# Dissolving a layer norm and routing stage into its neighbours, in a kernel of two attention and expert layers

## The chip, the cores and the metric

The kernel runs on one core of a Trainium2 chip. The metric is the device time of one execution in microseconds (us), the median of several runs. The core has five engines that run side by side, each from an instruction queue of its own and tied to the others by semaphores: TensorE (PE in the profile), VectorE (DVE), ScalarE (ACT), GpSimd (POOL) and SyncE (SP), which here only issues DMAs.

## What is computed

Two layers on `x` (8 x 256 rows of 256) with a context of the same shape; float32 throughout.

```python
x = x + _L0_xattn_ref(ctx_1024, _layernorm(x, axis=-1), ...)   # 16 heads of 64, 512 keys
x = x + _L0_ffn_ref(_layernorm(x, axis=-1), ...)               # the part around the change
x = x + _L1_xattn_ref(_layernorm(x, axis=-1), ctx_1024, ctx_1024, ...)
x = x + _L1_ffn_ref(_layernorm(x, axis=-1), ...)

def _L0_ffn_ref(...):                # x: 2048 rows of 256, 16 experts, F = 512
    logits = x @ w_router.T
    _, top_idx = jax.lax.top_k(logits, 1)
    mask = jax.nn.one_hot(top_idx, E).sum(axis=1)
    scores = jax.nn.sigmoid(logits) * mask
    masked_inputs = scores.T[:, :, None] * x[None, :, :]
    gate_up = jnp.einsum('eth,ehf->etf', masked_inputs, gate_up_proj)
    gate, up = jnp.split(gate_up, 2, axis=-1)
    expert_out = jnp.einsum('etf,efh->eth', up * silu(gate), down_proj)
    shared = silu(x @ w_gate.T) * (x @ w_up.T) @ w_down.T
    return shared + expert_out.sum(axis=0)
```

## The kernel before

`program` (L2116) runs stages one after the other, each a block of its own, with the semaphores cleared in between: `attend_latents`, `norm_and_route`, `run_mixture`, `attend_context`, `norm_and_gate`, `choose_and_run`. `x` lives in SBUF as 16 tiles of 128 rows; a batch is two tiles.

Products that need near float32 precision are made "threefold": each operand is split into a high part in fp32r (a copy by ACT) and a low part (the rest, by a subtraction on DVE or POOL), and three products are summed: high by high, high by low, low by high.

**`attend_latents`** (L67) goes through 8 batches of 8 steps, a step for each pair of heads; `batches` (L764) unrolls batches 0, 1, 6 and 7 and loops over 2 to 5. The order of work of each engine is written out by hand in its `step`. On PE a step makes the scores of four tiles (L297, L298), turns the exponentials (L307), projects k, q and v of what comes next (L255), and attends for the pair before (L321, L325). On DVE it takes four negative maxima (`maximum`, L603), the low part of k (L597) and of q (L590), copies of turned tiles (`set_odd`, L618), and the output of a pair (`set_out`, L625, L627). After each of the four maxima there is a slot, `between(r, j)`, for one of the 19 parts of `prepare`, which normalises the next batch: statistics, then an inverse root by Newton steps on small tiles, every instruction chained to the one before by a semaphore (`link`). The 19 parts fill the slots of steps 0 to 3 and three of step 4; the rest of step 4 and steps 5 to 7 are empty. In steps 4 and 5 `fill` (L582) follows slot 4 (PE turns the inputs for it, L333). At the end of step 2 `project_out` and `add` (L632) add the batch before to `x`; PE waits for `added` ahead of the q projection in step 3.

**`norm_and_route`** (L774) takes statistics of all 16 tiles, the root on ACT, and then per batch: normalise (DVE L729), turn (PE L741), copy (DVE L748), router logits in float32 (PE L836), a copy of the normalised rows (ACT L807), and the high and low parts `xT_h` (ACT L753) and `xT_l` (POOL L760). At its start it loads the weights of the shared expert and splits them (ACT L822, POOL L799).

**`run_mixture`** (L871) begins with three of the four groups (512 rows each) of the shared expert (EARLY = 3), in 12 steps `shared(n)`: products for gate and up of 6 matmuls each (L1028), silu on ACT, `hidden` on DVE (L1265), its high part on ACT (L1133) and low part on DVE (L1267); after each four steps comes `down` (48 matmuls, L1040; it starts in the step after), then `add`. Meanwhile DVE works out the routing in five parts, `route(0)` ahead of step 0 and `route(1)` to `route(4)` behind steps 0 to 3: part 0 finds the chosen expert (`hot_set`), PE counts (`count`, after step 0), part 3 gives each row its place (`row_set`), part 4 the expert of each block (`blocks_set`). ACT weighs the rows with their score, four tiles behind each of steps 0 to 3. POOL then scatters the rows of each tile to DRAM (L999), and SP loads weights for block 0 at `blocks_set`, for block 1 when `hidden_set` is 8, rows of three blocks when all is scattered, weights of block 2 when `hidden_set` is 12. Then 31 blocks of experts follow: turn rows (L1062), `expand` (L1069), `contract` (L1079).

## Time and profile before

| | us |
|---|---|
| median of 3 runs | 1676.8 |
| lowest and highest | 1675.89, 1679.48 |
| the profiled execution | 1679.78 |
| its span, first to last instruction | 1678.1 |
| TensorE busy | 1479.7 (88% of the span) |
| VectorE busy | 1017.5 (61%) |
| ScalarE busy | 879.1 (52%) |
| GpSimd busy | 458.8 (27%) |

The span is shorter than the execution by what lies around the program. Busy times of PE are modelled from pipelined matmuls, so a busy PE isn't one at its peak. The page has a line with the TensorE clock that the throttle granted, in 40 slices of the span; it is at full speed except around four stretches, one of them at 729 to 770 us. A row of the timeline reads: start, length, engine, line, operation, output <- inputs, form, number of instructions merged, and in brackets the idle time before it and what ended it.

### The profile page before, as it was taken

The page shows a single profiled execution, that of the slowest core. Times are in us where ns is not written, and L with a number is a line of the kernel's source. Part 1 is how long each engine was busy: PE and PEld are TensorE (multiplying, and loading weights), DVE is VectorE, ACT ScalarE, POOL GpSimd, SP SyncE. Part 2 cuts the span into 40 slices and gives each one's busy share as a digit, 9 for nine tenths or more (in the row PEclk, how much of TensorE's full clock was granted, in tenths as well). Part 3 has the DMA queues.
Part 4 walks back from the last instruction along what each step waited for, and adds up shares of the span by engine and source line. Part 5 has one row for each costly group of instructions (what it writes and reads, how often), then busy time and mean ns, then how long its engine had stood idle before and what let it go on. Part 6 is the DMA issues. An engine that isn't in the chain of part 4 may idle for free. (4 is left out here: it accounts for less than half of the span.)

```text
span 1678.1 us, 28402 instructions
## 1 busy us (share of the span) xinstructions
PE 1479.7 (88%) x9884; PEld 1201.2 (72%) x9884; DVE 1017.5 (61%) x2142; ACT 879.1 (52%) x2200; POOL 458.8 (27%) x395
## 2 busy tenths in 40 slices
PE   4899999999999999958999996699999629999996
PEld 3678777777777778747888885365655518888885
DVE  5877777777777876755311115377777654444452
ACT  2676767676767777835211113366666214445442
POOL 6110101010101010033200006222322015777874
PEclk9999999999999999977999998599999659999998
DMA  3300000000000000012489883000000223445442
GB/s 115 108 14 1 14 1 14 2 14 2 14 2 14 1 1 1 1 38 98 135 296 318 300 287 60 19 14 7 12 3 2 88 81 101 119 121 126 122 116 33
DMA packets 72255, 118.17 MB, mean 70 GB/s; under 512 B 6864, under 2 KB 52944, under 8 KB 72112
## 3 DMA queue, kind: packets, MB, share of 16 engines
q1 hardware_dynamic: 61408, 99.66, 18.4%
q0 software_dynamic: 10704, 16.65, 4.9%
q8 instruction: 83, 1.36, 0.3%
q14 instruction: 60, 0.49, 0.1%
HBM read 97.68 MB, written 18.61 MB: 69 GB/s over the span
## 5 line engine op out<-in xcount | busy, mean ns | idle before, releaser
L435 ACT ACTIVATE a_p<-a_s,a_negmax 128x512 f32<-128x512 f32 x256 | 176.0, 688 | 157.6 <-DVE a_negmax L603 115.9
L603 DVE TENSOR_REDUCE a_negmax<-a_s 128x1 f32<-128x512 f32 x256 | 176.1, 688 | 47.0 <-PE a_s L298 36.8
L207 POOL TENSOR_TENSOR a_o_l<-a_o,a_o_h 128x256 fp32r<-128x256 f32 x64 | 47.0, 735 | 559.8 <-ACT a_o_h L460 559.8
L1495 ACT ACTIVATE h_probs<-h_scores,h_negmax 128x256 f32<-128x256 f32 x256 | 117.8, 473 | 88.6 <-DVE h_negmax L1662 88.6
L307 PEld LDWEIGHTS a_t<-ident,a_p 128*128 128x128 f32 x1024 | 121.1, 140 | 52.9 <-issue 17.9
L307 PE MATMUL a_t<-ident,a_p 128*128 128x128 f32 x1024 | 157.5, 277 | 0.7 <-DVE a_pT L618 0.7
L1907 POOL TENSOR_TENSOR n_w_l<-n_raw,n_w_h 128x768 fp32r<-128x768 f32 x64 | 118.3, 1849 | 74.7 <-ACT n_w_h L1950 74.7
L597 DVE TENSOR_TENSOR a_k_hl<-a_k_p,a_k_hl 64x512 fp32r<-64x512 f32 x128 | 88.1, 688 | 71.6 <-ACT a_k_hl L418 70.5
L325 PE MATMUL a_out_p<-a_pT,a_v 128*64 128x256 f32 x1024 | 124.7, 386 | 0.0
L297 PE MATMUL a_s<-a_k_hl,a_q_hh 128*128 128x512 f32 x256 | 108.5, 424 | 8.9 <-ACT a_p L435 7.2
L1662 DVE TENSOR_REDUCE h_negmax<-h_scores 128x4 f32<-128x1024 f32 x64 | 78.1, 1221 | 55.3 <-PE h_scores L1589 55.3
L2088 DVE TENSOR_TENSOR n_hidden<-n_up,n_silu 128x512 f32<-128x512 f32 x64 | 44.3, 692 | 97.9 <-PE n_up L1992 93.6
L1600 PEld LDWEIGHTS h_turned<-ident,h_probs 128*128 128x128 f32 x512 | 55.8, 143 | 66.1 <-issue 48.0
L298 PE MATMUL a_s<-a_k_hl,a_q_l 128*128 128x512 f32 x256 | 101.3, 396 | 0.0
L412 ACT ACTIVATE a_q_hh<-a_q_p 64x256 fp32r<-64x256 f32 x256 | 95.9, 375 | 2.3
L325 PEld LDWEIGHTS a_out_p<-a_pT,a_v 128*64 128x64 f32 x1024 | 67.8, 136 | 38.4 <-issue 10.7
L2091 DVE TENSOR_TENSOR n_hid_l<-n_hidden,n_hid_h 128x512 fp32r<-128x512 f32 x64 | 63.3, 989 | 44.7 <-ACT n_hid_h L1971 44.7
L618 DVE COPY a_pT<-a_t 128x512 f32<-128x512 f32 x128 | 87.8, 686 | 2.6 <-PE a_t L307 0.7
L1600 PE MATMUL h_turned<-ident,h_probs 128*128 128x128 f32 x512 | 73.6, 286 | 13.5 <-DVE h_probsT L1672 13.4
L1966 ACT ACTIVATE n_silu<-n_gate 128x512 f32<-128x512 f32 x64 | 38.3, 598 | 84.2 <-PE n_gate L1992 84.2
L1334 DVE TENSOR_TENSOR e_hidden<-m_up,e_silu 128x512 f32<-128x512 f32 x31 | 21.4, 692 | 100.3 <-PE m_up L1069 100.3
L255 PE MATMUL a_v_p<-a_w_h,a_kvT_h 128*128 128x256 f32 x256 | 77.8, 304 | 4.8 <-POOL a_kvT_l L202 3.7
(325 smaller groups left out, 4294.3 us busy)
## 6 DMA issues: line engine op xcount, KB each, us to landing
e_w_in<-in_L_ffn_gate_up_proj SPq DMA_DIRECT2D x31, 1024.0 KB, 7.1
n_raw<-in_L_ffn_w SPq DMA_DIRECT2D x64, 384.0 KB, 3.0
e_w_out<-in_L_ffn_down_proj SPq DMA_DIRECT2D x31, 512.0 KB, 5.2
rows_in<-a_zeros SPq DMA_DIRECT2D x1, 3968.0 KB, 14.6
e_rows<-rows_in SPq DMA_DIRECT2D x31, 128.0 KB, 5.0
rows_out<-e_result POOLq DMA_DIRECT2D x31, 128.0 KB, 4.8
x<-in_x SPq DMA_DIRECT2D x8, 256.0 KB, 2.8
a_ctx_in<-in_ctx SPq DMA_DIRECT2D x8, 256.0 KB, 3.1
```

Of the source, the lines that this page charges most:

```text
L297: pe.matmul(scores[j % 2][:, :], q_hh[r % 2][:, h, rows], k_hl[r % 2][h][:, :], start=True, stop=False)
L298: pe.matmul(scores[j % 2][:, :], q_l[r % 2][:, h, rows], k_hl[r % 2][h][:, :], start=False, stop=True).then_inc(s_done, 1)
L307: ins = pe.transpose(turned_p[j % 2][:, c, :], probs[j][:, c * P:(c + 1) * P], g.ident[:, :])
L325: ins = pe.matmul(out_p[h * DH:(h + 1) * DH, 0, :], v[r // 2 % 2][:, c, at:at + DH], probsT[r % 2][h][:, c, :], start=(c == 0), stop=(c == ...
L412: ins = act.activation(q_hh[r % 2][half, h, :], q_p[halves[h], 0:S], ACT.Copy, scale=QSCALE)
L435: act.activation(probs[j][:, :], scores[j % 2][:, :], ACT.Exp, bias=negmax[:, j:j + 1], accum_out=total[:, r % 2, j % 2, j // 2:j // 2 + 1 ...
L597: ins = dve.tensor_tensor(k_hl[r % 2][h][halves[1 - h], :], k_p[half, :], k_hl[r % 2][h][half, :], ALU.subtract)
L603: dve.tensor_reduce(negmax[:, j:j + 1], scores[j % 2][:, :], AX.X, ALU.max, negate=True).then_inc(max_set, 1)
L618: dve.tensor_copy(probsT[r % 2][j // 2][:, :, P:2 * P], turned_p[1][:, :, :]).then_inc(odd_set, 1)
L1495: ins = act.activation(probs[s % 4][:, j, :], scores[s % 2][:, j // 2, j % 2, :], ACT.Exp, bias=negmax[:, s % 4, j:j + 1], accum_out=total ...
L1600: ins = pe.transpose(turned_p[i][:, j, c, :], probs[s % 4][:, 2 * i + j, c * P:(c + 1) * P], g.ident[:, :])
L1907: pool.tensor_tensor(w_l[c % RAWS][:, :], raw[c % RAWS][:, :], w_h[c % RAWS][:, :], ALU.subtract).then_inc(wl_set, 1)
```

## The change

The stage `norm_and_route` is gone, and its work is spread. In `attend_latents` each batch's final rows are also written to a tile `done` (an addition more), and `measure`, in nine parts, takes mean and inverse root of them in the slots that `prepare` leaves: slot 4 of step 4 and the slots of steps 5 and 6 of the next batch; for the last batch at the end. SP loads the shared expert's weights into the spare tiles of the attention. In `run_mixture` ACT and POOL split the weights, DVE normalises (`apply`), PE turns (`turn_x`) and makes the logits, threefold in fp32r instead of float32 (`find_logits`, 6 matmuls for each tile), ACT and DVE take the high and low parts, all between the products of steps 0 to 3. The logits lie in the PSUM tile that `down` writes too. `route(0)` to `route(4)` move behind steps 3 to 7, `count` behind `down(0)` in step 4, the weighing of rows to steps 4 to 7 and the split of the next attention's weights to steps 8 to 11.

```diff
-raw = [sb(f"a_raw{i}", [P, 3 * KC * N // 2]) for i in range(2)]
+raw = g.spare
...
+done, next_stats, next_mv = sb("a_done", [P, 2, D]), sb("a_next_stats", [P, 2, 6]), sb("a_next_mv", [P, 2, 2])
+next_var, next_tmp, next_guess = sb("a_next_var", [P, 2]), sb("a_next_tmp", [P, 2]), sb("a_next_guess", [P, 2], I32)
...
+        sp.wait_ge(w_ready, PIECES + OUT_PIECES)
+        for i, (w, name) in enumerate(zip(g.shared_raw, ("gate", "up"))):
+            sp.dma_start(w, io[f"L0_ffn_w_{name}_T"].rearrange("(c p) n -> p c n", p=P)).then_inc(stored, 16)
+        down_dram = io["L0_ffn_w_down_T"].rearrange("(i c p) n -> p i c n", i=2, p=P)
+        for i, w in enumerate(g.shared_raw[2:]):
+            sp.dma_start(w, down_dram[:, i]).then_inc(stored, 16)
-        sp.wait_ge(stored, 16)
+        sp.wait_ge(stored, 16 * 5)
     def _(pool):
...
     def _(dve):
-        PARTS = 19
+        PARTS, MEASURES = 19, 9
         def seed_root(n):
...
+        def measure(b, part):
+            at = bass.ds(2 * b, 2)
+            rstd_of = g.rstd[:, at]
+            if part == 0:
+                for t in range(2):
+                    ins = dve.bn_stats(next_stats[:, t, :], done[:, t, :])
+                link(ins)
+            elif part == 1:
+                for t in range(2):
+                    ins = dve.bn_aggr(next_mv[:, t, :], next_stats[:, t, :])
+                link(ins)
+                dve.tensor_copy(g.mean[:, at], next_mv[:, :, 0])
+                link(dve.tensor_scalar(next_var[:, :], next_mv[:, :, 1], EPS, None, ALU.add))
+            elif part == 2:
+                link(dve.tensor_scalar(next_guess[:, :], next_var[:, :].bitcast(I32), 1, None, ALU.logical_shift_right))
+                link(dve.tensor_scalar(next_guess[:, :], next_guess[:, :], -1, 0x5f3759df, ALU.mult, ALU.add))
+            else:
+                src = next_guess[:, :].bitcast(F32) if part < 5 else rstd_of
+                if part % 2:
+                    link(dve.tensor_tensor(next_tmp[:, :], src, src, ALU.mult))
+                    link(dve.tensor_tensor(next_tmp[:, :], next_tmp[:, :], next_var[:, :], ALU.mult))
+                else:
+                    link(dve.tensor_scalar(next_tmp[:, :], next_tmp[:, :], -0.5, 1.5, ALU.mult, ALU.add))
+                    link(dve.tensor_tensor(rstd_of, src, next_tmp[:, :], ALU.mult))
         def low_q(b, r):
...
         def add(b):
-            rows = g.x[:, bass.ds(2 * b, 2), :]
-            dve.tensor_tensor(rows, rows, q_p[:, :].rearrange("p (t d) -> p t d", t=2), ALU.add).then_inc(added, 1)
+            rows, sums = g.x[:, bass.ds(2 * b, 2), :], q_p[:, :].rearrange("p (t d) -> p t d", t=2)
+            link(dve.tensor_tensor(done[:, :, :], rows, sums, ALU.add))
+            dve.tensor_tensor(rows, rows, sums, ALU.add).then_inc(added, 1)
         def step(b, bp, first, last):
             def between(r, j):
-                if last < 2 and 4 * r + j < PARTS:
-                    prepare(b + 1, 4 * r + j)
+                if 4 * r + j < PARTS:
+                    if last < 2:
+                        prepare(b + 1, 4 * r + j)
+                elif not first and 4 * r + j < PARTS + MEASURES:
+                    measure(b - 1, 4 * r + j - PARTS)
             for r in range(PAIRS):
...
+        for part in range(MEASURES):
+            measure(NB - 1, part)
...
-def norm_and_route(nc, g, io):
...
 def run_mixture(nc, g, io):
...
-raw = [sb(f"g_raw{i}", [P, KC, D]) for i in range(4)]
+raw = [w[:, i * KC * D:(i + 1) * KC * D].rearrange("p (c n) -> p c n", c=KC) for w in g.spare for i in range(2)]
+router, router_h, router_l = (sb(f"r_router{i}", [P, KC, E], dt) for i, dt in enumerate((F32, F32R, F32R)))
+SPLITS = [(g.shared_h[i][:, :, :], g.shared_l[i][:, :, :], g.shared_raw[i]) for i in range(2)]
+SPLITS += [(g.shared_h[2][:, 2 * i:2 * i + 2, :], g.shared_l[2][:, 2 * i:2 * i + 2, :], g.shared_raw[2 + i]) for i in range(2)]
+logits = sum_ps[1][:, 0, :].rearrange("p (t e) -> p t e", e=E)
+r_in, sh_set, sl_set, rh_set, rl_set = sem("r_in"), sem("s_sh_set"), sem("s_sl_set"), sem("r_rh_set"), sem("r_rl_set")
+x_normed, x_turned, x_high, x_low, logits_done = sem("x_normed"), sem("x_turned"), sem("x_high"), sem("x_low"), sem("r_logits_done")
...
+        sp.dma_start(router[:, :, :], io["L0_ffn_w_router_T"].rearrange("(c p) e -> p c e", p=P)).then_inc(r_in, 16)
+        sp.wait_ge(sl_set, 4)
         for dst, name in zip(raw, ("Wq", "Wk", "Wv", "Wo")):
...
     def _(pool):
+        for i in range(len(SPLITS)):
+            high_w, low_w, raw_w = SPLITS[i]
+            pool.wait_ge(sh_set, i + 1)
+            pool.tensor_tensor(low_w, raw_w, high_w, ALU.subtract).then_inc(sl_set, 1)
+            if i == 1:
+                pool.wait_ge(rh_set, 1)
+                pool.tensor_tensor(router_l[:, :, :], router[:, :, :], router_h[:, :, :], ALU.subtract).then_inc(rl_set, 1)
...
+        def turn_x(b):
+            pe.wait_ge(x_normed, b + 1)
+            wait(pe, x_low, b - 1)
+            for kc in range(KC):
+                for t in range(2):
+                    ins = pe.transpose(small[b % 2][:, kc, t * P:(t + 1) * P],
+                                       g.xn[:, 2 * b + t, kc * P:(kc + 1) * P], g.ident[:, :])
+            ins.then_inc(x_turned, 1)
+        def find_logits(b):
+            pe.wait_ge(x_low, b + 1)
+            for t in range(2 * b, 2 * b + 2):
+                at = slice(t * P, (t + 1) * P)
+                passes = [(x, w, kc) for kc in range(KC)
+                          for x, w in ((g.xT_h, router_h), (g.xT_h, router_l), (g.xT_l, router_h))]
+                for k, (x, w, kc) in enumerate(passes):
+                    ins = pe.matmul(logits[:, t, :], x[:, kc, at], w[:, kc, :], start=(k == 0), stop=(k == len(passes) - 1))
+            if b == NB - 1:
+                ins.then_inc(logits_done, 1)
         def shared(n, first):
+            if n % FC == 0 and n // FC * 2 < NB:
+                pe.wait_ge(x_low, 2 * (n // FC) + 2)
+            if n == 0:
+                pe.wait_ge(sl_set, 1)
             product(gate_ps[n % 2], 0, n, gated)
+            if n < NB // 2:
+                if n == 0:
+                    pe.wait_ge(rl_set, 1)
+                find_logits(2 * n)
+                if 2 * n + 2 < NB:
+                    turn_x(2 * n + 2)
+            if n == 0:
+                pe.wait_ge(sl_set, 2)
             product(up_ps[n % 2], 1, n, upped)
+            if n < NB // 2:
+                find_logits(2 * n + 1)
+                if 2 * n + 3 < NB:
+                    turn_x(2 * n + 3)
             if n % FC == 0 and n > first:
+                if n == FC:
+                    pe.wait_ge(sl_set, 4)
+                    pe.wait_ge(hot_set, 1)
         def count():
...
+        turn_x(0)
+        turn_x(1)
         for n in range(FC * EARLY):
             shared(n, 0)
-            if n == 0:
+            if n == FC:
...
         for n in range(FC * EARLY, FC * GROUPS):
-        down(GROUPS - 1)
+        if EARLY < GROUPS:
+            down(GROUPS - 1)
         for b in range(NB):
...
+        def high_w(i):
+            act.activation(SPLITS[i][0], SPLITS[i][2], ACT.Copy).then_inc(sh_set, 1)
+        def take_high(b):
+            act.wait_ge(x_turned, b + 1)
+            act.activation(g.xT_h[:, :, b * S:(b + 1) * S], small[b % 2][:, :, :], ACT.Copy).then_inc(x_high, 1)
+        high_w(0)
+        act.wait_ge(r_in, 16)
+        act.activation(router_h[:, :, :], router[:, :, :], ACT.Copy).then_inc(rh_set, 1)
+        take_high(0)
+        high_w(1)
+        take_high(1)
+        high_w(2)
+        high_w(3)
         for n in range(FC * EARLY):
-            if n == 0:
+            if 2 * n + 2 < NB:
+                take_high(2 * n + 2)
+            if n == 4:
-            if n == 0:
+            if 2 * n + 3 < NB:
+                take_high(2 * n + 3)
+            if n == 4:
-            if n < 4:
-                weigh_rows(range(n * NT // 4, (n + 1) * NT // 4))
-            else:
-                if n == 4:
+            if n in range(4, 8):
+                weigh_rows(range((n - 4) * NT // 4, (n - 3) * NT // 4))
+            elif n >= 8:
+                if n == 8:
-                if n - 4 < len(splits):
-                    act.activation(splits[n - 4][0][:, :, :], raw[n - 4][:, :, :], ACT.Copy).then_inc(wh_set, 1)
+                if n - 8 < len(splits):
+                    act.activation(splits[n - 8][0][:, :, :], raw[n - 8], ACT.Copy).then_inc(wh_set, 1)
         for j in range(BLOCKS):
...
         def route(part):
             if part == 0:
-                dve.tensor_reduce(top[:, :], g.logits[:, :, :], AX.X, ALU.max).then_inc(top_set, 1)
+                dve.wait_ge(logits_done, 1)
+                dve.tensor_reduce(top[:, :], logits, AX.X, ALU.max).then_inc(top_set, 1)
-                link(dve.tensor_tensor(hot[:, :, :], g.logits[:, :, :], along(top[:, :], E), ALU.is_equal))
+                link(dve.tensor_tensor(hot[:, :, :], logits, along(top[:, :], E), ALU.is_equal))
...
         def scale_queries():
...
+        def apply(b):
+            for t in range(2 * b, 2 * b + 2):
+                ins = dve.tensor_scalar(g.xn[:, t, :], g.x[:, t, :], g.mean[:, t:t + 1], g.rstd[:, t:t + 1],
+                                        ALU.subtract, ALU.mult)
+            ins.then_inc(x_normed, 1)
+        def take_low(b):
+            dve.wait_ge(x_high, b + 1)
+            at = slice(b * S, (b + 1) * S)
+            dve.tensor_tensor(g.xT_l[:, :, at], small[b % 2][:, :, :], g.xT_h[:, :, at], ALU.subtract).then_inc(x_low, 1)
         def shared(n):
+            if 2 * n + 2 < NB:
+                take_low(2 * n + 2)
+                if 2 * n + 4 < NB:
+                    apply(2 * n + 4)
...
+            if 2 * n + 3 < NB:
+                take_low(2 * n + 3)
+                if 2 * n + 5 < NB:
+                    apply(2 * n + 5)
         def add(grp):
...
-        route(0)
+        for b in range(2):
+            apply(b)
+        for b in range(2):
+            take_low(b)
+        for b in range(2, 4):
+            apply(b)
         for n in range(FC * EARLY):
-            if n < 4:
-                route(n + 1)
-            elif n == 4:
+            if n in range(3, 8):
+                route(n - 3)
+            elif n == 8:
             if n % FC == 1 and n > FC:
...
-attend_latents(nc, g, io)
-clear_semaphores(nc)
-with ExitStack() as ctx:
+g.mean, g.rstd = keep(whole, "mean", [P, g.NT]), keep(whole, "rstd", [P, g.NT])
+ctx = ExitStack()
+with ctx:
+    g.spare = [keep(ctx, f"spare{i}", [P, 3 * g.KC * g.S]) for i in range(2)]
+    half = g.KC * g.F
+    g.shared_raw = [w[:, 0:half].rearrange("p (c n) -> p c n", c=g.KC) for w in g.spare]
+    g.shared_raw += [w[:, half:].rearrange("p (c n) -> p c n", c=2) for w in g.spare]
+    attend_latents(nc, g, io)
+    clear_semaphores(nc)
...
-        g.logits = keep(inner, "logits", [P, g.NT, g.E])
-        norm_and_route(nc, g, io)
-        clear_semaphores(nc)
```

## Rows read from the trace of the kernel before

**Rows 1.** Table of windows: stretch, us, busy time (instructions) per engine, clock, DMA share, GB/s
```profile
637.00:728.00 91.00, 85.94 (x617) 69.42 (x616) 57.43 (x108) 60.22 (x151) 8.03 (x11) 1.00 0.00 1
729.00:764.00 35.00, 20.19 (x96) 19.78 (x96) 23.91 (x62) 15.47 (x29) 17.21 (x11) 0.55 0.14 46
764.00:788.00 24.00, 19.39 (x74) 14.72 (x75) 16.71 (x50) 15.63 (x29) 4.14 (x7) 0.86 0.21 66
764.00:828.00 64.00, 57.16 (x291) 48.33 (x292) 30.01 (x71) 26.49 (x48) 22.38 (x24) 0.90 0.40 134
1070.00:1094.00 24.00, 22.15 (x79) 15.24 (x79) 8.23 (x10) 11.82 (x40) 9.78 (x10) 0.50 0.03 11
```

**Rows 2.** Timeline of DVE over the two changes of block
```profile
728.34 0.69 DVE L632 TENSOR_TENSOR x<-x,a_q_p 128x512 f32<-128x512 f32 x1 [7.30 <-PE a_q_p L255]
729.95 5.33 DVE L711 BATCH_NORM_STATS2 c_stats<-x 128x6 f32<-128x256 f32 x16 [0.92 <-PEq L2109]
735.31 1.17 DVE L714 BATCH_NORM_AGGREGATE c_mv<-c_stats 128x2 f32<-128x6 f32 x16
...
764.64 0.42 DVE L1218 TENSOR_REDUCE r_top<-logits 128x16 f32<-128x256 f32 x1 [3.69 <-PEq L2109]
```

**Rows 3.** Timeline of PE in the two stages after the attention
```profile
757.46 1.73 PE L836 MATMUL c_logit<-c_router,c_full 128*128 128x16 f32 x8
...
765.20 0.63 PE L1028 MATMUL m_gate<-xT_l,shared_h 128*128 128x512 f32 x1
765.63 0.63 PE L1028 MATMUL m_gate<-xT_h,shared_l 128*128 128x512 f32 x1
...
771.29 0.40 PE L1028 MATMUL m_gate<-xT_h,shared_l 128*128 128x512 f32 x1
...
786.00 0.39 PE L1040 MATMUL m_sum<-shared_h,s_hid_h 128*128 128x256 f32 x1 [1.80 <-DVE s_hid_l L1267]
...
827.91 0.39 PE L1062 MATMUL m_small<-ident,e_rows 128*128 128x128 f32 x2
```

**Rows 4.** Timeline of DVE: two chained small instructions of `prepare`
```profile
499.38 0.17 DVE L512 TENSOR_SCALAR a_var<-a_mv 128x2 f32<-128x2 f32 x1
499.58 0.17 DVE L513 TENSOR_SCALAR a_guess<-a_var 128x2 int32<-128x2 int32 x1
```

**Rows 5.** Timeline of PE: attends in steps 0, 1, 2, 5, 7 of batch 5, 0 of 6
```profile
471.85 0.38 PE L321 MATMUL a_out_p<-ident,a_inverses 128*128 128x128 f32 x2
...
482.97 0.41 PE L321 MATMUL a_out_p<-ident,a_inverses 128*128 128x128 f32 x2 [0.66 <-DVE a_pT L618]
...
493.29 0.41 PE L321 MATMUL a_out_p<-ident,a_inverses 128*128 128x128 f32 x2 [0.65 <-DVE a_pT L618]
...
529.38 0.41 PE L321 MATMUL a_out_p<-ident,a_inverses 128*128 128x128 f32 x2 [0.66 <-DVE a_pT L618]
...
549.52 0.38 PE L321 MATMUL a_out_p<-ident,a_inverses 128*128 128x128 f32 x2
...
558.90 0.38 PE L321 MATMUL a_out_p<-ident,a_inverses 128*128 128x128 f32 x2
```

**Rows 6.** Timeline of DVE ahead of `set_out`: step 5 of batch 5, and a clean step
```profile
530.23 0.86 DVE L590 SCALAR_TENSOR_TENSOR a_q_l<-a_q_p,a_q_hh 64x256 fp32r<-64x256 f32 x2 [0.35 <-ACT a_q_hh L412]
...
531.72 0.42 DVE L625 COPY a_inverse_T<-a_out_p 128x256 f32<-128x256 f32 x1
...
655.58 0.42 DVE L625 COPY a_inverse_T<-a_out_p 128x256 f32<-128x256 f32 x1 [0.57 <-PE a_out_p L325]
```

**Rows 7.** Timeline of POOL (split of weights, scatter), and a wait of SP's queue
```profile
734.64 6.95 POOL L799 TENSOR_TENSOR shared_l<-c_raw,shared_h 128x1024 fp32r<-128x1024 f32 x3 [12.34 <-ACT shared_h L822]
...
784.23 1.18 POOL L999 DMA_INDIRECT rows_in<-xn,row_of  x1 [18.56 <-DVE row_of L1248]
...
804.21 0.97 POOL L999 DMA_INDIRECT rows_in<-xn,row_of  x1 [0.30 <-issue]
...
SPq L964 <- DMA rows_in<-xn,row_of: 6.0, 1, 6.0
```

83 lines of the change are left out of this document (4 added, 79 removed).

## The prediction

> **What bounds the kernel now.** I read four views: the page for the stages, the table of windows for clock and busy shares, the timeline of each engine from 464 to 560 us and 640 to 830 us, and the waits of the stage from 764 us. The first attention is bound by TensorE: in its last 91 us PE is busy 86 at full clock [rows 1]. The stage the change removes is not: between 729 and 764 us PE is busy 20 of 35 us, at a mean clock of 0.55, only turning tiles and making logits [rows 1]. It starts 0.9 us after the last addition of the attention ends and hands over at 764.6 [rows 2]. The early groups of the shared expert run from there to 827.9, where the first rows of the experts are turned [rows 3]; PE is busy 57 of 64 us there [rows 1]. The gain can only come from 729.0 to 827.9; the bill is sent partly to the attention.
>
> **Removed.** From 729.03 (728.34 + 0.69) to 764.6 is 35.6 us: a block change of 0.92, then 34.6 us of stage [rows 2]. The block change stays, so the removal is worth 34.6.
>
> **Added at the end of the attention.** The last batch has nothing to hide under. First a second addition of 128x512 (into `done`), chained: 0.7, as the row of the existing one [rows 2]. Then nine parts: two statistics (16 took 5.33, so 0.7 for two [rows 2]), the aggregation with copy and the variance (0.6), two seed instructions and twelve Newton instructions, all chained, 0.20 apart [rows 4]: 2.8. Sum 4.9 us on the path.
>
> **Added inside the attention.** DVE's chain there is: attend (L321/L325) on PE, then `set_out`, `set_odd`, `maximum` of the next head pair, exp and two copies on ACT, `low_k`, `set_odd`, and the next attend. In a step with nothing extra attends are 9.38 apart (549.52 to 558.90), and this is also PE's own work [rows 5]. What happens when DVE gets small chained parts in all four slots is in the trace, since `prepare` does this: 471.85 to 482.97 is 11.12 and 482.97 to 493.29 is 10.32, so 1.74 and 0.94 are lost; four Newton parts take 4 x 0.42 = 1.7 us of DVE, and the step loses over half of it [rows 5]. The first slot lies in a wait of DVE and is free; slots 2 and 3 share 0.57 us of idle time ahead of `set_out` (655.58), slot 4 has no cover [rows 6]. Check: 0.84 - 0.57 + 0.42 = 0.69 against 0.94.
> The new parts go to slot 4 of step 4, and all slots of steps 5 and 6. Those steps are already late: 529.38 to 549.52 is 20.14 for two, 1.4 over, with `fill` in slot 4 and the turning of inputs on PE [rows 5]. Per batch in the loop: slot 4 of step 4, two statistics, 0.8, in full. Step 5: first slot free (a wait for ACT); slots 2 and 3, 0.84, less the 0.35 that DVE waits before `low_q` at 530.23 (ahead of 531.72 there is no idle left) [rows 6], so 0.5; slot 4, 0.45: 0.95. Step 6 by the measured 0.94, less some slack of the clean step 7: 0.8. The chained extra addition in step 2 delays the next `maximum` by 0.75; the chain of step 3 has about 0.25 to spare: 0.5. That is 3.05 for each of the four looped batches. The unrolled ones carry no address arithmetic; batches 1 and 6 I take at 2.4, batch 7, which has no `prepare` and starts from clean steps, at 1.9. Sum 12.2 + 4.8 + 1.9 = **19 us**. Bounds: if only the statistics show, 0.5 x 7, some 4 us; if every chained pair costs its time, 7 x 3.7, 26. I stay near the upper middle since rows 5 measure just such parts. The four weight DMAs on SP stand before the load of batch 2 and wait for a split long done by then; nothing is queued behind them that is due soon: 0.
>
> **The new front of the expert stage**, t from its start. Before, gate product 0 starts at 0.1. Now it waits for `x_low` 2. ACT: weight copy, router (landing some 2.3, bounded by the 2 of a small load and 6), copy of batch 0 (to 3.3), weight copy 1 (to 4.4), copy of batch 1 (5.0); DVE takes the low part to 5.8. POOL's low parts (6.95 for three, 2.3 each [rows 7]) end at 3.4 and 6.7 and are behind that for `gate` and just in time for `up`. So gate 0 starts at **5.9**.
> Steps 0 to 3 each have 12 matmuls of 512 columns: 0.43 apart at the low clock [rows 3], about half that at the full (0.23 with the gap), 5.1 or 2.8 in all, plus 24 logit matmuls of 16 columns, and 8 transposes in the first three (0.9 to 1.9 us). The logit matmuls in fp32r aren't in the trace; fp32 ones are 1.73 for 8 at the low clock, 0.22 each, 0.11 at the full [rows 3]; no less than 0.05, a quarter of the former, since these pass fp32 once instead of four times (an estimate). I take 0.075, 1.8 a step at the full clock. DVE gets per step, beside the pair of 0.69 us, two low parts (0.69 each) and two normalisations (0.7 each), 4.9 us, so PE, at 5.5, is just the later one. With step 0 all at the low clock: 5.9 + 10.3 + 5.5 + 5.5 + 4.5 = 31.7. The five parts of `route` are some 12 us of DVE: it is busy 16.7 us from 764 to 788 [rows 1], less four shared pairs of 1.4, plus the gaps between chained instructions. `route(0)`, 2.8 of them, comes after that and `down(0)` waits for `hot_set`: starts at **35.6**. Before it started at 786.00 - 764.6 = 21.4 [rows 3].
> From `down(0)` to the turning of rows: 42 us before [rows 3]. After: the same PE work, but `count` follows `down(0)`, and parts 1 to 3 of `route` (3.1, 3.1, 1.5) with the sum of group 0 (1.3) hold back `hidden` of steps 5, 6 and 7, on which gate 8 and `down(1)` wait: about 2 us each, against one such wait of the same kind before. I get 46, so t = **81.5**, against 63.3 before (827.91 - 764.6).
> The scatter: `row_set` comes at t = 55.7; 16 scatters stand 1.27 apart (784.23 to 804.21), SP waited 6.0 for their landing, and rows then took 2 [rows 7]: 28.6, so t = 84.3 by the rows; with the weights of blocks 0 and 1 loaded before the tail rather than in it, 80. I take 1 us of waiting: front **82.5**.
>
> **Sum** in the profiled execution: +19 + 4.9 - 34.6 + (82.5 - 63.3 = 19.2) = **+8.5**: expert start at 836.4 instead of 827.9. Everything behind is untouched; loads are issued by the experts' own progress. Span 1678.1 to 1686.6; the profiled run lies 1.7 above its span and 3 above the median, so the median goes from 1676.8 to **1685**.
>
> **Rivals.**
> 1. The new parts hide in the attention (loss about 4, the lower bound): +8.5 - 15 = -6.5, **1670**. For: DVE is busy only 57 of 91 us [rows 1], and a clean step follows. Against: rows 5. It decides if steps 5 to 7 lose under 1 us per batch. Chance 0.2.
> 2. TensorE stays at the low clock through steps 1 to 3: 2.3 more for each product pair and 1 to 1.5 for the small ones, 11 in all: **1696**. For: the mean clock was 0.55 from 729 to 764 under transposes and 16-column products, and 0.50 from 1070 to 1094 with PE busy 22 of 24 us [rows 1]. Against: step 0 in the trace, products only, raised it within some 5 us (a product of 0.63 at 765.2, of 0.40 at 771.3) [rows 3]. Chance 0.23.
> The Trainium skill (TensorE: Matmul & The Clock Gate, Part 4) says a transpose isn't counted as busy work by the clock's monitor; by that rule rival 2 is more likely, and the window of 0.55 agrees with it.
> 3. Chained instructions cost no more than unchained ones. Unchained aggregations stand 0.07 apart (16 in 1.17 [rows 2]); at that price a part is 0.15, the attention loses 10.5 and the tail 2.9: +8.5 - 8.5 - 2 = -2, **1675**. Against: chained ones of that size are 0.20 apart [rows 4]. Chance 0.05.
> The Trainium skill (VectorE: DVE Perf Modes, The DRAIN you can't avoid) says a semaphore after each instruction costs nothing extra; that is measured on large copies, and the rows of small ones disagree.
>
> **How the numbers follow.** Forecast (a net loss of 2 to 15) 0.52, rival 1 0.2, rival 2 0.23, rival 3 0.05. A difference under 0.2% (3.4 us) can't be told from none. Faster: rival 1, 0.2. Same: rival 3 and the lower edge of the forecast, 0.1. Slower: 0.7. Range 1670 to 1698; the forecast's own is 1679 to 1692.
>
> **What would show it.** The two steps of 20.14 in a looped batch take 22, and the one before them 0.8 more; first gate product 5.9 us after the block's start; `down(0)` 35 us after it; clock full again by gate 1; scatter done within a few us of `down(2)`. Wrong if the attention's last addition comes within 8 us of 728.3, or if the logit matmuls cost over 0.15 us.

## The result, and the profile after

The changed kernel is slower. Its median is 1690.5 us (1687.3 to 1697.1) against 1676.4 for the kernel before: a ratio of 1.0089, 95% interval 1.0053 to 1.0126, some 14 to 15 us. The profiled execution took 1687.3 us (span 1685.6), 7.5 more than that of before; it is the fastest of its runs, while the one profiled before was the slowest of its own, which is why the profiles differ by less than the medians. The direction and the time are as forecast (1685, range 1670 to 1698), but in the two profiles the sum under them holds two errors that nearly cancel, and they are the subject of what follows.

**The stages.** The table of windows of the changed kernel: stretch, us, busy time (instructions) of PE, PEld, DVE, ACT, POOL, clock, DMA share, GB/s. The lines answer to those of [rows 1]: the end of the attention, the last batch's moments, the new front of the expert stage, the part of it at full clock, and the stretch at the low clock behind the experts.

```profile
667.00:758.00 91.00, 83.86 (x588) 66.88 (x587) 59.42 (x124) 57.85 (x145) 7.34 (x10) 0.98 0.00 1
759.00:766.00 7.00, 0.27 (x3) 0.07 (x1) 4.98 (x23) 0.18 (x1) 0.00 (x0) 0.82 0.00 0
766.00:846.00 80.00, 71.20 (x419) 62.12 (x420) 43.15 (x95) 34.35 (x61) 29.33 (x29) 0.91 0.26 88
773.00:818.00 45.00, 41.46 (x265) 36.44 (x264) 26.14 (x65) 17.99 (x32) 2.34 (x6) 0.99 0.10 30
1050.00:1091.00 41.00, 15.79 (x62) 12.58 (x64) 20.33 (x76) 13.81 (x26) 15.30 (x15) 0.50 0.20 36
```

PE did 86 us of work in the last 91 us of the attention before, and does 84 now: it waits more. In the new front it is at full clock from 774 to 818.

**The attention.** PE's timeline, attends in steps 0, 4 (the one ahead of step 5), 5, 6 and 7 of batch 5 and 0 of batch 6 [rows 5]:

```profile
490.11 0.38 PE L330 MATMUL a_out_p<-ident,a_inverses 128*128 128x128 f32 x2
...
537.40 0.41 PE L330 MATMUL a_out_p<-ident,a_inverses 128*128 128x128 f32 x2 [0.66 <-DVE a_pT L653]
549.20 0.41 PE L330 MATMUL a_out_p<-ident,a_inverses 128*128 128x128 f32 x2 [0.66 <-DVE a_pT L653]
562.24 0.38 PE L330 MATMUL a_out_p<-ident,a_inverses 128*128 128x128 f32 x2
572.41 0.41 PE L330 MATMUL a_out_p<-ident,a_inverses 128*128 128x128 f32 x2 [0.62 <-DVE a_pT L653]
581.83 0.38 PE L330 MATMUL a_out_p<-ident,a_inverses 128*128 128x128 f32 x2
```

The two steps that took 20.14 take 572.41 - 549.20 = 23.21. From step 5 to 6 it is 13.04 where it was 10.75 (before, the attend of step 6 starts at 540.13), from 6 to 7 10.17 where it was 9.39. A looped batch loses 4.4 to 4.7 us; all attends together take 694.6 us instead of 666.4, 28.2 more.

What does PE wait for in between? Its first value projection for the next batch waits for GpSimd. First the changed kernel, then the kernel before, both PE's timeline in step 6 of batch 5:

```profile
560.24 0.38 PE L264 MATMUL a_v_p<-a_w_h,a_kvT_h 128*128 128x256 f32 x1 [1.25 <-POOL a_kvT_l L211]
```

```profile
538.13 0.38 PE L255 MATMUL a_v_p<-a_w_h,a_kvT_h 128*128 128x256 f32 x1 [0.63 <-POOL a_kvT_l L202]
```

The end of the chain was there already: DVE's first maximum of step 6, the exponential of it, then the high part of the second half of the next inputs on ACT (L412), its low part on GpSimd (L211), 1.27 us, and the projection. All of DVE's slots of step 5 lie ahead of that maximum. And one of the new instructions is five times as long as the next. DVE and GpSimd of the changed kernel:

```profile
549.13 0.82 DVE L610 TENSOR_SCALAR a_next_guess<-a_next_var 128x2 int32<-128x2 int32 x1
549.98 0.17 DVE L611 TENSOR_SCALAR a_next_guess<-a_next_guess 128x2 int32<-128x2 int32 x1
```

```profile
548.65 1.27 POOL L211 TENSOR_TENSOR a_kvT_l<-a_full,a_kvT_h 128x512 fp32r<-128x512 f32 x1 [5.47 <-ACT a_kvT_h L412]
...
558.85 1.26 POOL L211 TENSOR_TENSOR a_kvT_l<-a_full,a_kvT_h 128x512 fp32r<-128x512 f32 x1 [3.50 <-ACT a_kvT_h L412]
```

The instruction of 0.82 us on 128x2 numbers ends when GpSimd's ends (549.95 and 549.92). It does so in all six batches in which L211 runs beside it; in the last two it takes 0.17. In the kernel before, GpSimd's instruction stood at the same place, right behind the attend of step 5 (529.38), and no small instruction of DVE stood beside it:

```profile
528.84 1.27 POOL L202 TENSOR_TENSOR a_kvT_l<-a_full,a_kvT_h 128x512 fp32r<-128x512 f32 x1 [4.69 <-ACT a_kvT_h L403]
```

**Tail and front.** DVE's timeline over the change of block (it answers to [rows 2]), then PE's and POOL's in the front ([rows 3, 7]) and SP's wait:

```profile
759.31 0.69 DVE L667 TENSOR_TENSOR a_done<-x,a_q_p 128x512 f32<-128x512 f32 x1 [8.87 <-PE a_q_p L264]
760.03 0.69 DVE L668 TENSOR_TENSOR x<-x,a_q_p 128x512 f32<-128x512 f32 x1
...
764.56 0.16 DVE L619 TENSOR_TENSOR rstd<-rstd,a_next_tmp 128x2 f32<-128x2 f32 x1
765.84 1.38 DVE L1286 TENSOR_SCALAR xn<-x,mean,rstd 128x256 f32<-128x256 f32 x4 [1.12 <-PEq L2157]
...
770.46 4.37 DVE L1286 TENSOR_SCALAR xn<-x,mean,rstd 128x256 f32<-128x256 f32 x4
```

```profile
770.60 0.80 PE L988 MATMUL m_gate<-xT_h,shared_h 128*128 128x512 f32 x1 [1.99 <-DVE xT_l L1293]
...
800.10 0.36 PE L1000 MATMUL m_sum<-shared_h,s_hid_h 128*128 128x256 f32 x1 [0.63 <-issue]
...
817.34 0.50 PE L988 MATMUL m_gate<-xT_h,shared_h 128*128 128x512 f32 x1 [2.91 <-DVE s_hidden L1304]
...
845.90 0.38 PE L1063 MATMUL m_small<-ident,e_rows 128*128 128x128 f32 x2
```

```profile
820.43 1.18 POOL L959 DMA_INDIRECT rows_in<-xn,row_of  x1 [45.01 <-DVE row_of L1272]
...
839.95 0.97 POOL L959 DMA_INDIRECT rows_in<-xn,row_of  x1 [0.30 <-issue]
...
SPq L914 <- DMA rows_in<-xn,row_of: 14.8, 1, 14.8
```

From the start of the last batch's (first) addition to the next block's first instruction it is 6.53 us instead of 1.61. From there to the turning of rows it is 80.1 (765.8 to 845.9) instead of 63.3. The experts begin 18.0 us later than before.

### The profile page after: what moved, and what is told of

Read it like the earlier page. It is cut to its first block and busy times, and to the rows that moved or that the text cites. A ratio compares the mean times of both kernels' runs of the same rounds, so it can differ in the third digit from the quotient of the medians.

```text
span 1685.6 us, 28504 instructions
## 1 busy us (share of the span) xinstructions
PE 1477.5 (88%) x9916; PEld 1192.8 (71%) x9916; DVE 1043.7 (62%) x2273; ACT 872.6 (52%) x2184; POOL 448.4 (27%) x389
```

## The experiments

Ten more kernels ran, and the two of the change once more, on four occasions and three chips. Each ratio is to runs of the kernel before on the same occasion; the interval is 95%. Three of them ran once each, so that only their profiles are read: the kernel of experiment 6, the second of 7, and the kernel before in 8.

**1. All moments behind the attention**, and no second addition in it.

```diff
-                        elif not first and 4 * r + j < PARTS + MEASURES:
-                            measure(b - 1, 4 * r + j - PARTS)
...
-                    link(dve.tensor_tensor(done[:, :, :], rows, sums, ALU.add))
...
+                for t in range(g.NT):
+                    ins = dve.bn_stats(all_stats[:, t, :], g.x[:, t, :])
```

> The changed kernel, but nothing of the moments inside the attention: no second addition, no parts in the loop; all 16 statistics, the aggregations and one Newton chain for 16 columns follow the last addition. Theory (the whole loss is the attention's 28 us, of which the small chained DVE parts are the cause, while tail and front are as worked out): the attends of all eight batches stand as before (sums 71.8, 85.0, 87.1, 89.4, 87.0, 87.1, 85.0, 73.9), 28 less than in the changed kernel; the last addition to the next block grows from 6.5 to about 1.6 + 5.4 + 1.2 + 3.2 = 11.4; experts' start at 845.9 - 28 - 1 + 4.9 = 822, and the time is some 24 below the changed kernel's: 1666, 10 below the kernel before. Rival (the part behind the experts' start pays back what is lost ahead of it, as it paid back 10 us between the two profiles): half of it shows, 1676.

The attends are back: 667.3 us in all, 0.9 more than before (one dip of the clock in batch 3). In the timeline of DVE the moments stand after the last addition:

```profile
730.71 0.69 DVE L669 TENSOR_TENSOR x<-x,a_q_p 128x512 f32<-128x512 f32 x1 [7.32 <-PE a_q_p L266]
731.43 5.32 DVE L719 BATCH_NORM_STATS2 a_all_stats<-x 128x6 f32<-128x256 f32 x16
736.79 1.17 DVE L722 BATCH_NORM_AGGREGATE a_all_mv<-a_all_stats 128x2 f32<-128x6 f32 x16
...
742.64 3.42 DVE L1301 TENSOR_SCALAR xn<-x,mean,rstd 128x256 f32<-128x256 f32 x4 [1.49 <-PEq L2172]
```

From the addition to the next block 11.9 us (11.4 expected). Ratio 0.9971 (0.9953 to 0.999), that is 5 us under the kernel before and, by the ratios, 20 under the changed one. The moments and the addition cost what the theory says in the attention; the experts' start in this profile was 836.6, not 822, for a reason that experiments 8 and 9 look at. The changed kernel's 1.0089 was measured where that reason was absent; where it was present, in experiment 8, its ratio is 1.0141, and against that this kernel is 29 us faster and the next one 33.

**2. Statistics in the loop, one Newton chain at the end.** Only two statistics, two aggregations and a copy stay inside, in the first slots of steps 5 and 6; the second addition goes, and the one left is chained, with one small instruction behind it that signals PE; one chain of 16 columns follows the last addition.

```diff
-                        elif not first and 4 * r + j < PARTS + MEASURES:
-                            measure(b - 1, 4 * r + j - PARTS)
+                        elif not first and (r, j) in ((5, 0), (6, 0)):
+                            moments(b - 1, r - 5)
...
-                    link(dve.tensor_tensor(done[:, :, :], rows, sums, ALU.add))
-                    dve.tensor_tensor(rows, rows, sums, ALU.add).then_inc(added, 1)
+                    link(dve.tensor_tensor(rows, rows, sums, ALU.add))
+                    dve.tensor_copy(next_tmp[:, 0:1], g.eps[:, 0:1]).then_inc(added, 1)
```

> The changed kernel with only the statistics and the aggregation (with one copy) of each batch inside the attention, in the first slots of steps 5 and 6, where DVE waits for ACT in any case, and one Newton chain for all 16 columns behind the last addition; the addition is made once. Theory: a part in the first slot is hidden, so the attends cost under 0.5 us per batch more than before (the single chained addition some 0.1, the copy 0.2): the attention loses 2 to 4 us instead of 28; the tail is 1.6 + 0.7 + 0.3 + 0.2 + 3.2 = 6. Time some 25 below the changed kernel: 1664 to 1666. Rival (any chained DVE instruction in steps 5 and 6 costs its time, wherever it stands): 7 x 1.6 = 11 us in the attention: 1673.

The attends take 668.6 us, 2.2 more than before, about 1.0 of it one clock dip in batch 3 (one interval of 13.18 instead of 11.66, the next 10.58 instead of 11.10). Steps 5 to 7 are as before, 10.75 and 9.39; the interval into step 4 is 10.25 to 10.31 instead of 10.03 to 10.06, which the chaining of the addition costs. From addition to block 6.36. Ratio 0.9945 (0.992 to 0.9969), 24 us under the changed kernel. Work in the first slot is free, as forecast; it is the other slots that cost.

**3. `fill` ahead of the part of slot 4**, in steps 4 and 5.

```diff
-                        between(r, 3)
...
-                        if r in (4, 5) and last < 2:
-                            fill(b + 1, r - 4)
+                        if r in (4, 5):
+                            if last < 2:
+                                fill(b + 1, r - 4)
+                            between(r, 3)
```

> The changed kernel with the order of two calls swapped in steps 4 and 5: fill first, then the part of slot 4. Theory (from step 5 to step 6 the attends stand 13.04 apart instead of 10.75 because project_q of the next batch waits for filled, and fill stands behind DVE's parts): that interval falls by 0.4 to 0.9 in each looped batch, by 0.4 in batches 1 and 6, and step 4 to 5 by up to 0.3; in all 4 us off: 1686.5. Rival (the late one is DVE's own maximum and set_out; fill is in the same queue, so its order doesn't matter): intervals within 0.2 of the changed kernel's, 1690.5.

Ratio 1.0133 (1.0101 to 1.0165); the attends take 698.1, 3.5 more than in the changed kernel. `fill` does end 1.0 us sooner behind the attend of step 5 (6.0 instead of 7.0), and DVE's next maxima 0.3 sooner, but the interval from step 5 to 6 is 14.03 in batch 5. PE's timeline:

```profile
562.61 0.57 PE L264 MATMUL a_v_p<-a_w_h,a_kvT_h 128*128 128x256 f32 x1 [1.26 <-POOL a_kvT_l L211]
562.99 0.42 PE L264 MATMUL a_v_p<-a_w_l,a_kvT_h 128*128 128x256 f32 x1
```

The wait for GpSimd is the same 1.26, and behind it the matmuls stand 0.21 apart instead of 0.12: the granted clock is 0.5 from 562.2 to 565.6. In batch 2, with the clock full, the interval is 13.07 (12.70 in the changed kernel), and `fill` ended 0.65 sooner there too. So `filled` wasn't what PE was late for, and this theory of mine falls. In batches 3 to 5 the clock fell for 3.4 us behind the wait, which costs 1.3 to 1.5 in that interval, counted from the maximum as in the table of experiment 7. The changed kernel's own profile has no such dip inside the loop, but one at 753.2 to 756.6, in the last output projection: from the last attend to the addition it takes 12.1 instead of 10.5.

**4. One addition.** The statistics read `x` itself.

```diff
-                    link(dve.tensor_tensor(done[:, :, :], rows, sums, ALU.add))
-                    dve.tensor_tensor(rows, rows, sums, ALU.add).then_inc(added, 1)
+                    link(dve.tensor_tensor(rows, rows, sums, ALU.add))
+                    dve.tensor_copy(next_tmp[:, 0:1], g.eps[:, 0:1]).then_inc(added, 1)
```

> The changed kernel without the second addition: the statistics read the rows of x themselves, and the one addition is chained (one small instruction behind it signals PE). Theory (the second addition is on the path: the interval into step 3 grew by 0.5 and the next by 0.27): each of seven batches gets 0.6 to 0.75 back, the tail 0.6: in all 5.5, 1685. Rival (the loss there is the chaining, the wait for the write to land, not the 128x512 of work): 0.2 back per batch, 1689.

The interval into step 3 falls from 15.55 to 15.08 in the loop and the one into step 4 stays at 10.3: 0.5 us per batch, between the two expectations. A low clock from 371.9 to 378.7 takes 1.9 back in batch 3 (14.96 from step 5 to 6), and smaller losses in batches 5 (13.38) and 7 the rest, so that the attends sum to 694.4 as in the changed kernel. Ratio 1.0118 (1.0086 to 1.015): in the time nothing can be told from the changed kernel.

**5. The seed by `tensor_tensor`.**

```diff
-                        link(dve.tensor_scalar(next_guess[:, :], next_var[:, :].bitcast(I32), 1, None, ALU.logical_shift_right))
+                        link(dve.tensor_tensor(next_guess[:, :], next_var[:, :].bitcast(I32), one_i[:, :], ALU.logical_shift_right))
...
```

> The changed kernel with the two seed instructions of a batch's inverse root as tensor_tensor with small constant tiles instead of tensor_scalar: as many chained instructions, same slot. Theory (the first of them takes 0.82 us instead of 0.17 in six batches because it holds still until GpSimd's low part of the inputs, L211, is over; a tensor_tensor doesn't need what GpSimd holds): it takes under 0.3 us in all batches, and the attend interval from step 4 to 5 or 5 to 6 falls by 0.4 to 0.65 in six batches: 3 us off the changed kernel. Rival (any DVE instruction waits there, since the wait is for the semaphore of the instruction before): 0.8 as before and no gain.

```profile
549.92 0.81 DVE L611 TENSOR_TENSOR a_next_guess<-a_next_var,a_one_i 128x2 int32<-128x2 int32 x1
```

```profile
549.44 1.27 POOL L212 TENSOR_TENSOR a_kvT_l<-a_full,a_kvT_h 128x512 fp32r<-128x512 f32 x1 [5.47 <-ACT a_kvT_h L413]
```

Still 0.81, still to GpSimd's end: the form of the instruction doesn't matter, both forms are held. The attends sum to 695.7, and to 695.2 in the changed kernel on the same occasion: no gain; the ratios are 1.011 (1.009 to 1.013) and 1.0141 (1.012 to 1.0161). DVE's copies and reductions of PSUM beside the same instruction of GpSimd keep their 0.69. The Trainium skill (SBUF — State Buffer, Who interferes with whom) says that DVE and GpSimd share one pair of ports under an exclusive lock, and that it touches a `tensor_scalar` in its fast mode as well as a `tensor_tensor` with both inputs in SBUF; the traces agree in that both instructions were held, though they don't show the mode. What this experiment couldn't tell is lock from semaphore; the next one moves the instruction.

**6. The second slot of step 5 left empty.**

```diff
+                SLOTS = [(4, 3), (5, 0), (5, 2), (5, 3), (6, 0), (6, 1), (6, 2), (6, 3), (7, 0)]
...
-                        elif not first and 4 * r + j < PARTS + MEASURES:
-                            measure(b - 1, 4 * r + j - PARTS)
+                        elif not first and (r, j) in SLOTS:
+                            measure(b - 1, SLOTS.index((r, j)))
```

> The changed kernel with the second slot of step 5 left empty; the parts behind it move one slot on, the last into the first slot of step 7. Theory (the 0.82 us instruction waits for GpSimd's L211, which runs in that slot alone): none of the small instructions takes 0.8; the interval from step 5 to 6 falls from 12.70 to about 12.0 in the four looped batches, steps 6 to 7 stay at 10.17, step 7 loses nothing, since its first slot is free. Rival (the late one behind is GpSimd's low part of the second input half, for which TensorE waits, and DVE has caught up until then): under 0.2 off.

```profile
546.95 0.17 DVE L611 TENSOR_SCALAR a_next_guess<-a_next_var 128x2 int32<-128x2 int32 x1
```

```profile
545.21 0.41 PE L330 MATMUL a_out_p<-ident,a_inverses 128*128 128x128 f32 x2 [0.66 <-DVE a_pT L654]
...
557.00 0.38 PE L330 MATMUL a_out_p<-ident,a_inverses 128*128 128x128 f32 x2
```

The same instruction takes 0.17 in all eight batches. From step 5 to 6 it is 11.79 instead of 13.04 (11.82 instead of 12.70 in the even batches), and steps 6 to 7 and 7 to 0 are as they were (10.15, 9.42). The part costs more than its length: 0.9 to 1.25 us came back for 1.0 us of DVE moved. All attends: 688.4, 6.2 less. So in the second slot of step 5 a part was paid in full, the hold included. The 0.34 by which the odd batches lost more is gone too: it was a gap of 0.55 instead of 0.21 us ahead of `fill` in step 5, which the traces show but don't explain.

**7. The high part ahead of the exponential**, in step 6, in the kernel of experiment 2 and alone in the changed kernel.

```diff
+                        if r == 6 and last < 2:
+                            high_kv(b + 1, 1 - bp, 1)
                         exponent(b, r, 0)
                         if prev:
                             set_even(*prev, 2)
-                        if r == 6 and last < 2:
-                            high_kv(b + 1, 1 - bp, 1)
```

> The kernel with one Newton chain at the end (the statistics alone in the loop), and in step 6 ScalarE's high part of the next batch's second input half (L412) ahead of the first exponential instead of behind it. Theory (the end of the chain of step 6 is: DVE's maximum, that exponential, the high part on ScalarE, the low part on GpSimd, 1.27 us, and then the value projection of the next batch, which waits for it; that is why DVE's parts of step 5, which come ahead of this maximum, were paid in full): the interval from step 5 to 6 falls from 10.75 to 9.6 or less in the four looped batches and from 10.55 in batches 1 and 6: 6 to 8 us off, 0.4% under the kernel with the chain at the end. Rival (PE's own work of that step, with the turned inputs of the next batch, is 10.5): no change.

> The changed kernel, all its parts in place, with ScalarE's high part (L412) ahead of the first exponential of step 6. Theory (of the 2.0 to 2.3 us that step 5 to 6 lost in the change, about half is there because the chain maximum, exponential, high part, low part on GpSimd, value projection starts behind all four slots of step 5): the interval falls from 12.70 or 13.05 to 11.7 or less, by more than the 0.67 that the same edit gave without the parts. Rival (with the parts DVE itself is the last, whoever waits for GpSimd): 12.0 to 12.7, at most the same 0.67 off.

In the first, step 5 to 6 goes from 10.75 to 10.07 (PE's attends of batch 5 below), all attends from 668.6 to 663.8, less than in the kernel before; ratio 0.9932 (0.9912 to 0.9953). In the second it goes from 12.70 to 12.05 and from 13.04 to 12.37: the same 0.65, not more, and step 6 to 7 gives 0.14 of it back (10.31 after 10.17).

```profile
528.66 0.41 PE L332 MATMUL a_out_p<-ident,a_inverses 128*128 128x128 f32 x2 [0.65 <-DVE a_pT L665]
538.73 0.41 PE L332 MATMUL a_out_p<-ident,a_inverses 128*128 128x128 f32 x2
```

So PE's wait for GpSimd was on the path and worth 0.65 us a batch before the change and after it, and once it is gone DVE's parts still cost 2.0 to 2.3: the rival was right. The parts delay DVE's own chain, and GpSimd's low part was only the last to hand it on.

The profiles show where the delay passes. Read from the attend of step 5, with the clock full:

| | DVE's first maximum of step 6 | attend of step 6 |
|---|---|---|
| kernel before | 4.64 | 10.74 |
| experiment 6 | 5.70 | 11.82 |
| changed kernel, even and odd batches | 6.60, 6.94 | 12.70, 13.04 |
| experiment 3, batch 2 | 6.95 | 13.07 |
| experiments 4 and 5, batch 5 | 7.28, 7.25 | 13.38, 13.36 |
| experiment 7, first kernel | 4.64 | 10.08 |
| experiment 7, second, even and odd batches | 6.60, 6.93 | 12.04, 12.37 |

The attend follows that maximum by 6.10 to 6.12 us, and by 5.44 with the early split, whatever stood in the slots. What the parts cost in step 5 is what they put ahead of the maximum in DVE's queue.

The second kernel moved the hold as well. GpSimd's low part now ran beside a Newton instruction of step 6, and this one took 1.27 us instead of 0.16, in all six batches:

```profile
553.73 1.27 DVE L616 TENSOR_TENSOR a_next_tmp<-a_next_tmp,a_next_var 128x2 f32<-128x2 f32 x1
```

```profile
553.71 1.27 POOL L211 TENSOR_TENSOR a_kvT_l<-a_full,a_kvT_h 128x512 fp32r<-128x512 f32 x1 [1.60 <-ACT a_kvT_h L412]
```

The hold follows GpSimd's instruction to another instruction and another slot, so it isn't the semaphore of the instruction before. It lay in a first slot and was over in time: the maximum behind it was done at 555.81, and ScalarE, whose exponential needs that maximum, was busy until 556.07. In the first kernel the copy of the statistics took 1.10 us at the same place.

**8. The stall in the front.** The profiles of experiments 1 to 4 had 86 to 89 us from the first gate product to the copy of the first expert rows; the changed kernel's first profile had 76.7. So both kernels ran again, unchanged, on a further chip.

> The changed kernel once more, word for word, on the chip on which the first experiments ran. There four kernels with the changed kernel's front had, in their profiles, 86 to 89 us from the first gate product to the copy of the first expert rows, where the first profile of the changed kernel had 76.7: ScalarE stood still twice, for 2.7 and 3.6 us beyond its last visible releaser, and TensorE with it, while the experts' first weights were loaded, and the clock fell for 6.8 us behind that. Theory (ScalarE's stall is a matter of the chip or the run, not of the edits, and explains why the profiles differ by 7.5 us and the medians by 14): the stall is there again, front 86 to 89, span about 1697, ratio to the kernel before 1.007 to 1.012. Rival (it comes with the edits' other instruction stream): front 76.7, span near 1688.

> The kernel before once more, word for word, on the chip of the experiments. Theory (the stall of ScalarE and VectorE while the experts' first weights land comes only with the changed front, where their issue and the last shared groups run beside each other later in the stage): no stall, 63 us from the first gate product to the copy of the first expert rows, as in the first profile (64.7). Rival (it is the chip's and both kernels have it): 66 or more.

The stretch took 89.8 us in the changed kernel and 73.8 in the kernel before (64.7 in its first profile); the attends differ by 28.6 us, as before. Ratio 1.0141 (1.012 to 1.0161). ACT's timeline, the changed kernel on this chip, then in its first profile:

```profile
826.09 0.57 ACT L1131 ACTIVATE s_silu<-m_gate 128x512 f32<-128x512 f32 x1
835.23 0.63 ACT L1137 ACTIVATE s_hid_h<-s_hidden 128x512 fp32r<-128x512 f32 x1 [8.57 <-remote]
```

```profile
822.92 0.57 ACT L1131 ACTIVATE s_silu<-m_gate 128x512 f32<-128x512 f32 x1
828.02 0.63 ACT L1137 ACTIVATE s_hid_h<-s_hidden 128x512 fp32r<-128x512 f32 x1 [4.52 <-PE m_sum L1000]
```

And DVE's in the kernel before on this chip:

```profile
804.47 0.69 DVE L1265 TENSOR_TENSOR s_hidden<-m_up,s_silu 128x512 f32<-128x512 f32 x1 [6.75 <-issue]
```

ACT and DVE stand still, 4 us and more beyond anything the trace shows them waiting for, while the weights of the first two expert blocks come in at 400 GB/s. Both kernels have it, and it depends on the occasion: where the kernel before had a median of 1682 to 1683 every profile showed it, where it had 1676 to 1677 none did. It isn't the chip alone: one chip had it at one time (experiments 1 to 4) and not at another (6, the second of 7 and the first of 9). It costs the changed kernel 13 us of that stretch and the kernel before 9.

**9. Late weights.** To see whether the weights' loads are behind that stall, they were moved back, in the first kernel of experiment 7. A second kernel waits for the eleventh hidden tile instead of the twelfth ahead of the first load.

```diff
                 sp.wait_ge(blocks_set, 1)
+                sp.wait_ge(hidden_set, FC * EARLY)
                 load_weights(0)
-                sp.wait_ge(hidden_set, FC * EARLY - 4)
-                load_weights(1)
                 sp.wait_ge(scattered, 16 * NT)
                 for j in range(AHEAD):
                     load_rows(j)
-                sp.wait_ge(hidden_set, FC * EARLY)
+                load_weights(1)
                 load_weights(2)
```

> The kernel with the early split and one Newton chain, and the weights of the first two expert blocks loaded only when the last hidden tile of group 2 is made (they were issued 25 us earlier, when block_expert was there); the rows are loaded between them. Theory (ScalarE and VectorE stand still 5.7, 2.5 and 4.4 us while those 3 MB fill the DMA engines at 400 GB/s, since something they need comes by the same engines; their instructions, which no view shows): no wait of ScalarE put down to 'remote' and none of VectorE to 'issue' in that stretch; from the first gate product to the copy of the first expert rows 79 to 83 us instead of 92; the time 8 us less, 1662, 0.988 of the kernel before. Rival (the stalls come from the scatter, or from anything else but the weights): they stay, and block 0 waits for its weights besides: 1672 or more.

> The kernel with the late weights, the first of them one hidden tile sooner (at the eleventh instead of the twelfth). In its profile ScalarE and VectorE had no unexplained wait in the front, but nor had two kernels of the same call with the weights at their old place, so that the late weights weren't shown to be the cure. Theory (the stalls come where the weights' loads are queued while the shared groups still run, on an occasion on which they come at all, which the kernel before shows by a median of 1682 or more instead of 1676): no unexplained wait over 2 us, and about 1.3 us less than the kernel with the late weights, since block 0 waited 1.5 us for its weights: 1659 and a ratio of 0.990 where the kernel before has 1676, 1660 to 1664 and 0.987 to 0.989 where it has 1682. Rival (the stalls follow the occasion, not the weights): with the kernel before at 1682 or more the waits are there, 2 to 5 us each, and the ratio is 0.993.

No stall in either, and 78.1 and 77.1 us for the stretch. But two kernels with the weights at their old place, experiment 6 and the second of experiment 7, ran on the same occasion as the first of these and had none either (79.6 and 77.8), and the second of these ran on an occasion with the kernel before at 1676.7. So the cause isn't shown. Ratios: 0.9908 (0.9882 to 0.9935) and 0.9909 (0.9896 to 0.9923), 1660.7 and 1661.0 us: the tile sooner gave nothing that shows. They are the fastest of the study, 15 us under the kernel before and, by the ratios, 30 under the changed one; how much of the last step is the weights' place, and how much the occasion, stays open, since the kernel that they build on ran where the stall was.

## Why the prediction came out as it did

**Added inside the attention, +19: the failed term, it measured 28.2.** By its steps, for a looped batch:
- slot 4 of step 4, 0.8: measured 0.78 (11.80 after 11.02). Right.
- step 6, 0.8: 10.17 after 9.39. Right.
- the second addition, 0.5: measured 0.50 into step 3, which experiment 4 gave back, and 0.27 into step 4, 0.77. The 0.27 stays with one chained addition (experiments 2 and 4) and is gone with one unchained (10.04, experiment 1), so it belongs to the chaining, not to the second addition.
- step 5, 0.95: measured 2.0 to 2.3. This is the step that failed. I took 0.35 off for DVE's idle time ahead of `low_q` [rows 6], but every slot but the first was paid in full: 0.42 + 0.42 + 0.45 = 1.29, and 0.65 for the instruction held by GpSimd, 1.94 in all. The held one I didn't think of, though GpSimd's L202 stands in the trace of before where the new part would go; experiment 6 took the part out and got 0.9 to 1.25 back. The odd batches of the loop lose 0.34 more, by the gap ahead of `fill` that experiment 6 names. Experiment 7 adds that PE's wait for GpSimd has no share in the loss: without it the loss is the same. Rows 5 held a warning: of the two steps with four parts one lost 1.74, and I took neither of the two for step 5.

Beside the sum: the attention began 1.1 us later, and the clock dip of the last output projection cost 1.6. From first instruction to last addition it is 31.0 against 19.

**Tail, +4.9**: 6.53 - 1.61 = 4.92, instruction for instruction as costed from [rows 4]. The experiments with one chain of 16 columns took 0.21 an instruction: from 2 to 16 columns the price is that of the instruction and its chaining, not of its columns.

**Removed, -34.6**: as read.

**Front, 82.5: it measured 80.1.** Gate 0 started 4.8 after the block, 5.9 forecast. The logit matmuls (24 in 2.5 us) stand 0.104 apart, not 0.075, and steps 1 to 3 took 6.3, 6.3 and 5.5 us, not 5.5, 5.5 and 4.5; step 0 took 7.7 and not 10.3, since the clock was full again at 773.7, three microseconds into it. `down(0)` at 34.3 (35.6), the tail of `route` and the waits behind it 45.8 us (46). The scatter was late for SP, 14.8 us of wait, but the rows were there when `down(2)` ended: my 1 us of waiting was 0.

So the experts' start came at 18.0 instead of 8.5 behind: 31.0 + 4.9 - 34.6 + 16.8, to within 0.1.

**"Everything behind is untouched": false by 10.5 us in the profile, in the helpful direction.** The end is 7.5 behind, not 18.0. 3.2 us came back in the experts, 2.2 up to the first projection of the context attention, and 5.1 in its course: it began 26.7 us before the end of the low clock in the kernel before (1067.4, low until 1094.1) and 11.0 before it in the changed one (1080.1, until 1091.1). That isn't shown to be a gain of the change. In the two profiles of experiment 8 the low stretch there was 44 us before (3.4 + 41.0) and 58 after (3.4 + 54.6), the other way round, and the spans differ by 23.0. The mean clock and the time of a run go together, for one kernel: the changed kernel's four first runs had 1685.6, 1687.5, 1690.2 and 1695.4 at mean clocks of 0.955, 0.954, 0.952 and 0.950. A single profile is good to some 5 us here. The forecast span of 1686.6 and the measured 1685.6 agree by this luck; by the medians the change costs 14 us where I had forecast 8.

**Rivals.** 1 (hidden in the attention): no; steps 5 to 7 lose 3 us a batch. 2 (low clock in steps 1 to 3): no; it was at full from 773.7 to 818.0, with the transposes and logit matmuls between the products. The Trainium skill's rule named beside that rival isn't contradicted: 12 products stood around the 8 transposes of each step. Transposes and logits alone, without the products, had a mean clock of 0.55 before [rows 1]. 3 (chained as cheap as unchained): no, 0.20 apart as in [rows 4].

## What to carry to other kernels

"A slot where the engine waits" is free only if nothing behind it is on the path: follow the chain from each slot to the next stage's wait, through the other engines, before counting its idle time. Keep a dozen small chained instructions out of the slots of a tight loop that stand ahead of such a chain: the same moments cost 28 us as seven small chains in the loop (with the second addition that fed them) and 3 us as one chain over all columns behind it, while the statistics, in a truly free slot, cost nothing that could be seen. And put small SBUF work of DVE where GpSimd isn't in the middle of a long instruction.
